# Slot tiles of a routed feed-forward layer: the up bias, the PSUM banks, the weight slots and the ring of slot rows

## Chip, core and metric

One core of a Trainium2 chip runs the program. The metric is device time of one execution in microseconds, lower is better. The engines are TensorE (PE), VectorE (DVE), ScalarE (ACT), GpSimd (POOL) and SyncE (SP); 16 DMA engines move data for all of them.

## What is computed

Four layer groups follow each other on a tensor of 8 sequences x 256 tokens x 128 features: state-space, linear, windowed, delta-rule and causal attention layers, and feed-forward layers between them. The change bears on one of these, the feed-forward layer of the first group, which the program runs twice for each half of the batch. Its shapes in the reference are

```python
B, S, H, F, E, K = (2, 256, 128, 512, 8, 2)

def _ffn(x, wi, bi, wo, bo):
    return jax.nn.selu(x @ wi + bi) @ wo + bo
```

A gate of that form (gate_wi, gate_wo) is evaluated for every token; its output picks the token's top 2 choices, and a choice below 8 names one of 8 experts with weights exp_wi (128 x 512), exp_wo (512 x 128) and biases exp_bi (512), exp_bo (128). Each chosen expert is applied to the token, and the results come back weighted. All is fp32; small bf16 operands are used where they are exact, or as three bf16 parts of one fp32 number.

## The kernel before

Everything after the inputs is held on chip. Two streams, a and b, each work on half of the sequences; stream a has PSUM banks 0 to 3, b has 4 to 7. A layer is a function that gives one generator per engine; each generator waits (`yield pe.wait_ge(signal, n)`) and issues. The planner `Weave` joins them: each engine has one instruction queue in order, and Weave picks at every step the generator that could go on first by its own due times, which come from the costs in `Lane` (L115 to L232). So a cost in `Lane` changes nothing that is computed, but the order in which the two streams' work stands on each engine, in the whole program.

`experts` is the routed layer. One call treats 8 token tiles of 128 of its stream (two sequence pairs). In steps:

- the gate, in 8 units (`GATE`), then the routing on DVE (`route`): one-hot marks, counts by a product with ones, places, the number of the expert of each of 23 slot tiles (`rows`, and `picked`, which marks in 96 rows the expert of a tile), and for each choice its `slots` row.
- POOL scatters the token rows to DRAM by `slots`, 16 indirect DMAs a stream; SP loads them back sorted by expert: `xg`, 23 tiles of 128 rows, six transfers of 4 tiles (the last of 3), all sent before the first tile.
- 23 slot tiles (`SLOT_TILES`). For tile j: `turn(q)` transposes four tiles of rows at a time into bank 3, `keep_x` on ACT copies them to `xgT`; `up(j)` makes the 128 x 512 hidden layer in bank j % 2, as four chunks of 128 columns, each a weight product and a bias product (96 rows hold three bf16 parts of the biases, in parts of 32, and `picked` chooses the expert); `grow` on ACT takes the exp, DVE makes SELU of it in two steps (`fall`, `selu`) into `hidden`; `down(j)` is four weight products and a bias product into bank 2; `keep_y` on ACT copies it out. The order on TensorE in one stream is up(j+1), down(j).
- the weights of tile j, 512 KB, come to slot j % 3 of `ring_a` or `ring_b`. SP reads the expert's number from `rows` (`value`, a TENSOR_LOAD and register steps) and sends the load for j+3 once down(j) is done.
- y goes to DRAM in groups of four tiles, POOL gathers the rows back, 16 indirect DMAs a stream, and DVE adds them to x with the weights of the choice.

`ready` prepares the bias parts once, in `m.bias16`. In the traces L148 is the line of every product, L157 of a transpose, L166 of an ACT step, L179, L182, L185 and L188 of DVE's, L216 and L221 of POOL's scatter and gather, L231 of SP's transfers.

## Time and profile before

| | us |
|---|---|
| median of 3 runs | 2962.91 (2961.7 to 2963.11) |
| the profiled execution | 2957.25 |
| its span, first to last instruction | 2955.9 |
| busy in it: PE | 2287.9 (77%) |
| DVE | 1866.6 (63%) |
| ACT | 1356.9 (46%) |
| POOL | 695.9 (24%) |

The busy times are averages over some fifteen layers with different limits. The routed layer's slot tiles run in two stretches of the span, near 384 to 560 us and 668 to 850 us. In the page's slices of 74 us these are the ones where the DMA engines are busy after the start. A busy TensorE counts as busy while its pipeline drains, so neighbouring rows overlap, and the time that one product holds the engine is the distance between two starts.

### The profile page before, as it was taken

Reading aid. Unit: us, or ns where it says so; the run is one execution under the profiler, and the core shown is the slowest. Engines: PE = TensorE matmul, PEld = TensorE weight load, DVE = VectorE, ACT = ScalarE, POOL = GpSimd, SP = SyncE. Lnnn points to the kernel's source line nnn. Section 1 sums busy time; section 2 is a strip of 40 time slices with the busy share of each in tenths; the row PEclk is TensorE's granted clock in tenths of the full one; section 3 lists DMA queues with packets and bytes.
Section 4 is the critical chain, followed back from the end, with each engine's and each line's share of the span. In section 5 each row is a group of like instructions: output and inputs, shape, how many; then the busy total and the mean of one; then the engine's idle time right before and its main releaser. Section 6 shows DMA issues by size and latency. Waiting matters only on the chain. (4 is left out here: it accounts for less than half of the span.)

```text
span 2955.9 us, 40949 instructions
## 1 busy us (share of the span) xinstructions
PE 2287.9 (77%) x15598; PEld 1476.6 (50%) x15598; DVE 1866.6 (63%) x3594; ACT 1356.9 (46%) x2546; POOL 695.9 (24%) x610
## 2 busy tenths in 40 slices
PE   4777839574948887885888689766778989779889
PEld 1222439454934544453586368445455554555554
DVE  6989824493438978879898899753562242652331
ACT  4545304231427877873652464344334333435342
POOL 2727340404042212216591066000010100100000
PEclk9989969786969998996897699778789999899899
DMA  4000047304832111110000000202000000000000
GB/s 175 0 0 1 1 134 234 99 1 152 241 93 87 43 33 40 40 33 5 0 1 1 0 1 1 70 1 68 13 1 1 1 2 1 8 1 1 1 1 7
DMA packets 70708, 117.80 MB, mean 40 GB/s; under 512 B 9616, under 2 KB 46224, under 8 KB 70160
## 3 DMA queue, kind: packets, MB, share of 16 engines
q1 hardware_dynamic: 64112, 104.69, 12.0%
q0 software_dynamic: 4096, 8.40, 0.9%
q8 instruction: 123, 2.02, 0.3%
q10 hardware_dynamic: 2304, 2.10, 0.3%
q14 instruction: 73, 0.60, 0.1%
HBM read 84.61 MB, written 16.78 MB: 34 GB/s over the span
## 5 line engine op out<-in xcount | busy, mean ns | idle before, releaser
L185 DVE SCALAR_TENSOR_TENSOR conv<-conv_in,held_l1a,conv 128x512 f32<-128x512 f32 x288 | 244.2, 871 | 29.4 <-ACT conv L166 26.4
L179 POOL TENSOR_TENSOR long<-long,product 128x512 f32<-128x512 f32 x136 | 214.1, 1593 | 198.9 <-ACT product L166 190.4
L209 POOL MEMSET wide_q<- 128x1536 f32 x8 | 11.0, 1379 | 887.1 <-DVE stream_b L182 837.3
L179 POOL TENSOR_TENSOR part<-state,c_rows 128x512 f32<-128x512 f32 x128 | 161.1, 1285 | 72.1 <-issue 53.0
L179 POOL TENSOR_TENSOR qk<-conv,held_const 128x512 f32<-128x512 f32 x64 | 92.3, 1443 | 349.4 <-DVE conv L185 349.4
L182 DVE TENSOR_SCALAR grown<-grown 128x512 f32<-128x512 f32 x92 | 39.6, 430 | 210.6 <-ACT grown L166 163.7
L148 PE MATMUL ps<-part,held_const 128*128 128x512 f32 x256 | 147.1, 659 | 13.3 <-POOL part L179 8.4
L191 DVE TENSOR_TENSOR_SCAN state<-decay,ps 128x512 f32<-128x512 f32 x128 | 146.9, 1193 | 0.0
L188 DVE TENSOR_REDUCE wide_q<-ps 128x4 f32<-128x512 f32 (+1 forms) x128 | 113.5, 950 | 49.8 <-PE ps L148 49.8
L166 ACT ACTIVATE probs<-ps 128x768 f32<-128x768 f32 x128 | 96.5, 808 | 88.2 <-PE ps L148 88.0
L148 PE MATMUL ps<-yn,nT 128*128 128x192 f32 (+2 forms) x640 | 115.6, 313 | 20.3 <-DVE yn L179 17.6
L166 ACT ACTIVATE grown<-ps,held_route 128x512 f32<-128x512 f32 x92 | 63.3, 688 | 135.1 <-PE ps L148 94.6
L179 DVE TENSOR_TENSOR x<-x,ps 128x512 f32<-128x512 f32 x44 | 30.1, 685 | 132.7 <-PE ps L148 128.3
L194 DVE COPY outT<-ps 128x256 f32<-128x256 f32 x64 | 27.0, 422 | 135.1 <-PE ps L148 134.7
L148 PE MATMUL ps<-a,held_l3f 128*128 128x512 f32 x256 | 111.7, 593 | 0.5 <-DVE a L185 0.4
L148 PE MATMUL ps<-b,held_l3f 128*128 128x512 f32 x256 | 111.3, 592 | 0.0
L148 PEld LDWEIGHTS ps<-yn,nT 128*128 128x128 f32 x640 | 95.9, 198 | 27.4 <-issue 17.9
L166 ACT ACTIVATE product<-v_in,held_l1b 128x512 f32<-128x512 f32 x136 | 92.2, 714 | 8.0 <-POOL long L179 6.1
L166 ACT ACTIVATE probs<-ps,k_inv 128x192 f32<-128x192 f32 (+1 forms) x256 | 81.2, 397 | 30.5 <-PE ps L148 28.3
L148 PE MATMUL ps<-bc,pick 96*128 96x512 bf16 x128 | 50.8, 403 | 52.2 <-DVE state L191 45.5
L157 PE MATMUL ps<-held_const,stream_a 128*128 128x128 f32 x108 | 29.3, 400 | 77.7 <-DVE stream_a L182 77.6
L166 ACT ACTIVATE c_rows<-ps 128x512 f32<-128x512 f32 x64 | 38.2, 597 | 109.7 <-PE ps L148 103.7
(503 smaller groups left out, 6135.2 us busy)
## 6 DMA issues: line engine op xcount, KB each, us to landing
ring_a<-in_experts SPq DMA_DIRECT2D x46, 512.0 KB
ring_b<-in_experts SPq DMA_DIRECT2D x46, 512.0 KB
turned<-conv SPq DMA_DIRECT2D x256, 64.0 KB
ring<-lags SPq DMA_DIRECT2D x64, 128.0 KB
held_l3f<-in_l3f SPq DMA_DIRECT2D x1, 2824.0 KB
xg<-rows_x_a SPq DMA_DIRECT2D x10, 256.0 KB
xg<-rows_x_b SPq DMA_DIRECT2D x10, 256.0 KB, 5.2
rows_y_a<-y SPq DMA_DIRECT2D x10, 256.0 KB, 5.4
```

Of the source, the lines that this page charges most:

```text
L148: ins = self.real.matmul(out, lhsT, rhs, **kw)
L157: return self.array(self.real.transpose(out, a, ident), 0.109)
L166: return self.sent(self.real.activation(out, a, func, **kw), 0.13 + columns(out) / 1150, 0.14)
L179: return self.vector(self.real.tensor_tensor(out, a, b, op), columns(out), out, a, b)
L182: return self.vector(self.real.tensor_scalar(out, a, p, q, *ops), columns(out) // 2 + 40, out, a)
L185: return self.vector(self.real.scalar_tensor_tensor(out, a, p, b, first, second), columns(out) + 60, out, a, b)
L188: return self.sent(self.real.tensor_reduce(out, a, axis, op, **kw), 0.065 + columns(a) / 960, 0.13)
L191: return self.sent(self.real.tensor_tensor_scan(out, a, b, first, one, two), 0.04 + columns(out) / 480, 0.13)
L194: return self.vector(self.real.tensor_copy(out, a), columns(out), out, a)
L209: return self.vector(self.real.memset(out, value), columns(out) // 2, out)
```

## The change

For the slot tiles of `experts`:

- The up bias is one product per tile. `lifted`, made once per call on DVE (96 x 23 x 128, bf16), is the bias table times `picked`; the table now lies with its four chunks in four rows of an expert's part (8 experts x 4 chunks = 32 rows). The product has `lifted` of tile j as its stationary operand and `chunk16`, which marks a row's chunk, spread to 512 columns, as the moving one.
- `up` and `turn` take three banks in turn, in the order in which they are used; down has bank 3. up(j+2) stands ahead of down(j), no longer up(j+1).
- `W_RING` is 4.
- `xg` is a ring of three groups of four tiles: three loads are sent ahead, the others each when the turn of the group three before it is done.
- Four costs in `Lane` are raised: scatter, gather, value, dma_start.
- `ready` splits the two bias tables apart; a group `biases` holds them and lies in the ring's memory, `route` is smaller; `m.ones` is 128 wide and takes the place of `every_row`.

```diff
     def scatter(self, table, at, a):
-        self.engine.free += 1.0
+        self.engine.free += 1.27
...
     def gather(self, out, table, at):
-        self.engine.free += 1.0
+        self.engine.free += 1.27
...
     def value(self, a, top):
-        self.engine.free += 0.3
+        self.engine.free += 0.7
         return self.real.value_load(a, min_val=0, max_val=top)
 
     def dma_start(self, out, a):
-        self.engine.free += 0.1
+        self.engine.free += 0.35
...
-W_RING = 3
+W_RING = 4
+X_RING = 3
 CHUNK = 4
-X_GROUP = [0, 0, 1, 1, 1, 1]
+STARTS = range(CHUNK, SLOT_TILES, CHUNK)
...
-               picked=([P, SLOT_TILES], BF16), slot=[P, CHOICES], miss=[P, CHOICES], slots=([P, CHOICES], U32))
+               picked=([P, SLOT_TILES], BF16), lifted=([P, SLOT_TILES, P], BF16), slot=[P, CHOICES], miss=[P, CHOICES], slots=([P, CHOICES], U32))
...
-    xg = first.place([P, SLOT_TILES, P], name="xg")
+    xg = first.place([P, X_RING * CHUNK, P], name="xg")
...
+    uses = [("turn", 0), ("up", 0), ("up", 1)]
+    for j in range(SLOT_TILES):
+        uses += [("up", j + 2)] * (j + 2 < SLOT_TILES) + [("turn", (j + 3) // CHUNK)] * (j + 3 in STARTS)
+    bank_turn, bank_up = ({k: at % 3 for at, (what, k) in enumerate(uses) if what == name} for name in ("turn", "up"))
+    freed = {use: (s.kept_x, k + 1) if what == "turn" else (s.hidden, GATE + k + 1)
+             for use, (what, k) in zip(uses[3:], uses)}
+    down_out = st.ps(3)[:, 0:P]
+    up_bank = lambda u: u % 2 if u < GATE else bank_up[u - GATE]
...
-        pe.matmul(totals, w.every_row, marks, start=True, stop=True).then_inc(s.counted)
+        pe.matmul(totals, m.ones[:, :], marks, start=True, stop=True).then_inc(s.counted)
...
         def turn(q):
             at, n = SLICES[q]
-            yield pe.wait_ge(R.x_loaded[X_GROUP[q]], 16 * X_GROUP.count(X_GROUP[q]) * (done + 1))
-            if q:
-                yield pe.wait_ge(s.kept_x, q)
+            yield pe.wait_ge(R.x_loaded[q % X_RING], 16 * (x_before[q % X_RING] + q // X_RING + 1))
+            if q == 0:
+                yield pe.wait_ge(s.slots, 1)
             else:
-                yield pe.wait_ge(s.logits, len(every))
+                yield pe.wait_ge(*freed["turn", q])
             for i in range(n):
-                mm = pe.transpose(st.tiles(3)[:, i, :], xg[:, at + i, :], m.ident)
+                mm = pe.transpose(st.tiles(bank_turn[q])[:, i, :], xg[:, q % X_RING * CHUNK + i, :], m.ident)
             mm.then_inc(s.turn)
 
         def up(j):
             W = R.ring[:, j % W_RING, :]
+            out = st.ps(bank_up[j])
             yield pe.wait_ge(s.kept_x, j // CHUNK + 1)
             yield pe.wait_ge(R.w_loaded[j % W_RING], w_at(j))
-            if j >= 2:
-                yield pe.wait_ge(s.hidden, GATE + j - 1)
-            elif j == 0:
-                yield pe.wait_ge(s.slots, 1)
-                yield pe.wait_ge(s.picked, 1)
+            if j == 0:
+                yield pe.wait_ge(s.logits, len(every))
+                yield pe.wait_ge(s.picked, 2)
+            elif j >= 2:
+                yield pe.wait_ge(*freed["up", j])
             for c in range(FC):
-                out = tile(st.ps(j % 2), c)
-                pe.matmul(out, tile(W, c), tile(b.xgT[:, j // CHUNK % 2, :], j % CHUNK), start=True, stop=False)
-                mm = pe.matmul(out, tile(m.bias16[0:SPLIT, :], c), pick(j), start=False, stop=True)
-            mm.then_inc(s.up)
+                pe.matmul(tile(out, c), tile(W, c), tile(b.xgT[:, j // CHUNK % 2, :], j % CHUNK), start=(c == 0),
+                          stop=False, skip_group_check=True)
+            pe.matmul(out.rearrange("p (c n) -> p c n", c=FC), b.lifted[0:SPLIT, j, :],
+                      m.chunk16[0:SPLIT, :].unsqueeze(2).to_broadcast([SPLIT, FC, P]), start=False, stop=True,
+                      skip_group_check=True).then_inc(s.up)
 
         def down(j):
             W = R.ring[:, j % W_RING, :]
             hidden = b.hidden[:, j % FC, :]
-            yield pe.wait_ge(s.hidden, GATE + j + 1)
             if j:
                 yield pe.wait_ge(s.y_kept, j)
             for c in range(FC):
-                pe.matmul(st.ps(2)[:, 0:P], tile(hidden, c), tile(W, FC + c), start=(c == 0), stop=False)
-            pe.matmul(st.ps(2)[:, 0:P], pick(j), tile(m.bias16[0:SPLIT, :], FC), start=False, stop=True
-                      ).then_inc(s.y_made)
+                pe.matmul(down_out, tile(hidden, c), tile(W, FC + c), start=(c == 0), stop=False)
+            pe.matmul(down_out, pick(j), m.bias_down[0:SPLIT, :], start=False, stop=True).then_inc(s.y_made)
 
         yield from turn(0)
         yield from up(0)
+        yield from up(1)
         for j in range(SLOT_TILES):
-            if j % CHUNK == 1 and j // CHUNK + 1 < len(SLICES):
-                yield from turn(j // CHUNK + 1)
-            if j + 1 < SLOT_TILES:
-                yield from up(j + 1)
+            if j + 2 < SLOT_TILES:
+                yield from up(j + 2)
+            yield pe.wait_ge(s.hidden, GATE + j + 1)
+            if j + 3 in STARTS:
+                yield from turn((j + 3) // CHUNK)
             yield from down(j)
...
         for u in range(GATE):
             yield from grow(u, m.bias_grown[:, u % FC:u % FC + 1])
         yield from keep_x(0)
         yield from grow(GATE, w.ln_alpha)
+        yield from grow(GATE + 1, w.ln_alpha)
         for j in range(SLOT_TILES):
-            if j % CHUNK == 1 and j // CHUNK + 1 < len(SLICES):
-                yield from keep_x(j // CHUNK + 1)
-            if j + 1 < SLOT_TILES:
-                yield from grow(GATE + j + 1, w.ln_alpha)
+            if j + 2 < SLOT_TILES and j + 2 not in STARTS:
+                yield from grow(GATE + j + 2, w.ln_alpha)
+            if j + 3 in STARTS:
+                yield from keep_x((j + 3) // CHUNK)
+            if j + 2 in STARTS:
+                yield from grow(GATE + j + 2, w.ln_alpha)
             yield from keep_y(j)
...
             ve.tensor_scalar(b.picked[0:SPLIT, :], b.expert[0:SPLIT, :], float(E - 1), w.own_expert[0:SPLIT, :],
                              ALU.min, ALU.is_equal).then_inc(s.picked)
+            yield ve.wait_ge(s.picked, 1)
+            ve.tensor_tensor(b.lifted[0:SPLIT, :, :], m.bias_up[0:SPLIT, :].unsqueeze(1).to_broadcast([SPLIT, SLOT_TILES, P]),
+                             b.picked[0:SPLIT, :].unsqueeze(2).to_broadcast([SPLIT, SLOT_TILES, P]), ALU.mult
+                             ).then_inc(s.picked)
             yield ve.wait_ge(*own)
             slot = step(ve.tensor_reduce(b.slot[:, :], b.running[:, :, :].rearrange("p e c -> p c e"), X, ALU.add))
...
-        yield sp.wait_ge(m.bias_ready, 6)
+        yield sp.wait_ge(m.bias_ready, 12)
         yield sp.wait_ge(s.rows, 1)
         for j in range(W_RING):
             load(j)
         yield sp.wait_ge(R.scattered, 16 * CHOICES * (done + 1))
-        for q, (at, n) in enumerate(SLICES):
-            sp.dma_start(xg[:, at:at + n, :], R.x[at * P:(at + n) * P, :].rearrange("(t p) d -> p t d", p=P)
-                         ).then_inc(R.x_loaded[X_GROUP[q]], 16)
+        def load_x(q):
+            at, n = SLICES[q]
+            to = q % X_RING * CHUNK
+            sp.dma_start(xg[:, to:to + n, :], R.x[at * P:(at + n) * P, :].rearrange("(t p) d -> p t d", p=P)
+                         ).then_inc(R.x_loaded[q % X_RING], 16)
+
+        for q in range(X_RING):
+            load_x(q)
         for j in range(SLOT_TILES):
             if j + W_RING < SLOT_TILES:
                 yield sp.wait_ge(s.y_made, j + 1)
                 load(j + W_RING)
             q = j // CHUNK
             at, n = SLICES[q]
+            if j == at and q + X_RING < len(SLICES):
+                yield sp.wait_ge(s.turn, q + 1)
+                load_x(q + X_RING)
...
-        whole = w.expert_bias[0:SPLIT, :]
         step = Steps(m.bias_ready)
-        yield step(ve.tensor_scalar(whole[:, FC * P:], whole[:, FC * P:], 1.0 / SELU_SCALE, None, ALU.mult))
-        yield step(ve.tensor_copy(m.bias16[0:SPLIT, :], whole))
-        yield step(ve.tensor_tensor(m.bias_rest[0:SPLIT, :], whole, m.bias16[0:SPLIT, :], ALU.subtract))
-        yield step(ve.tensor_copy(m.bias_mid[0:SPLIT, :], m.bias_rest[0:SPLIT, :]))
-        yield step(ve.tensor_copy(m.bias16[32:64, :], m.bias_mid[32:64, :]))
-        yield step(ve.tensor_tensor(m.bias16[64:96, :], m.bias_rest[64:96, :], m.bias_mid[64:96, :], ALU.subtract))
+        yield step(ve.tensor_scalar(w.expert_bo[0:SPLIT, :], w.expert_bo[0:SPLIT, :], 1.0 / SELU_SCALE, None, ALU.mult))
+        for whole, out in ((w.expert_bi, m.bias_up), (w.expert_bo, m.bias_down)):
+            yield step(ve.tensor_copy(out[0:SPLIT, :], whole[0:SPLIT, :]))
+            yield step(ve.tensor_tensor(m.bias_rest[0:SPLIT, :], whole[0:SPLIT, :], out[0:SPLIT, :], ALU.subtract))
+            yield step(ve.tensor_copy(m.bias_mid[0:SPLIT, :], m.bias_rest[0:SPLIT, :]))
+            yield step(ve.tensor_copy(out[32:64, :], m.bias_mid[32:64, :]))
+            yield step(ve.tensor_tensor(out[64:96, :], m.bias_rest[64:96, :], m.bias_mid[64:96, :], ALU.subtract))
+        yield step(ve.tensor_copy(m.chunk16[0:SPLIT, :], w.own_chunk[0:SPLIT, :]))
...
```

Left out: the same renaming at the places that use the banks (`grow`, `keep_x`, `keep_y`, `selu`), the memory layout and the host's tables.

What stands on TensorE in the middle of the slot tiles, where both streams run. Before, the end of an up of a, the down of a, the start of an up of b (xgT is the transposed x, ring the weights, picked with bias the bias product, hidden the SELU's output; an up has four such pairs):

```order
L148 MATMUL ps<-xgT_153,ring_a_58 128x128
L148 MATMUL ps<-picked_169,bias_9_57 128x128
L148 MATMUL ps<-ring_a_58,hidden_152 128x128 x4
L148 MATMUL ps<-bias_9_57,picked_169 128x128
L148 MATMUL ps<-xgT_470,ring_b_59 128x128
L148 MATMUL ps<-picked_486,bias_9_57 128x128
```

And now, a whole up and down of a, and of b:

```order
L148 MATMUL ps<-xgT_156,ring_a_60 128x128 x4
L148 MATMUL ps<-chunk_59,lifted_173 128x512
L148 MATMUL ps<-ring_a_60,hidden_155 128x128 x4
L148 MATMUL ps<-down_58,picked_172 128x128
L148 MATMUL ps<-xgT_475,ring_b_61 128x128 x4
L148 MATMUL ps<-chunk_59,lifted_492 128x512
L148 MATMUL ps<-ring_b_61,hidden_474 128x128 x4
L148 MATMUL ps<-down_58,picked_491 128x128
```

An up is now four products in a row and one of 512 columns; the two streams still take turns, and the up that stands ahead of a down is that of two tiles later.

On DVE, at the end of stream a's routing in the first of the two layers, before (rows is what SP reads, picked marks the experts, slot and slots lead to the scatter):

```order
L182 TENSOR_SCALAR rows_168<-expert_167 1x23
L179 TENSOR_TENSOR running_161<-running_161,onehot_160 128x128
L182 TENSOR_SCALAR picked_169<-expert_167,held_route_56 96x23
L179 TENSOR_TENSOR used_479<-running_478,held_route_56 128x64
L188 TENSOR_REDUCE slot_170<-running_161 128x16
L179 TENSOR_TENSOR weight_159<-top_154,both_156 128x16
```

And now:

```order
L182 TENSOR_SCALAR rows_171<-expert_170 1x23
L179 TENSOR_TENSOR running_164<-running_164,onehot_163 128x128
L182 TENSOR_SCALAR picked_172<-expert_170,held_route_56 96x23
L179 TENSOR_TENSOR used_484<-running_483,held_route_56 128x64
L179 TENSOR_TENSOR lifted_173<-up_57,picked_172 96x2944
L188 TENSOR_REDUCE slot_174<-running_164 128x16
```

The multiply of 2944 columns a row stands between picked and slot.

On SP, behind the first weights of both streams, in the first of the two layers, before (xg is the load of slot rows, four tiles each; rows_168 is a's table of experts):

```order
L226 TENSOR_LOAD rows_485
L226 ISA x2
L231 ISA
L231 DMA ring_b_59<-in_experts 128x1024
L231 DMA xg_175<-rows_x_a 128x4x128 x5
L231 DMA xg_175<-rows_x_a 128x3x128
L226 TENSOR_LOAD rows_168
L226 ISA x2
```

And now, where one more load of each stream stands ahead:

```order
L226 TENSOR_LOAD rows_490
L226 ISA x2
L231 ISA
L231 DMA ring_b_61<-in_experts 128x1024
L231 DMA xg_179<-rows_x_a 128x4x128 x3
L226 TENSOR_LOAD rows_171
L226 ISA x2
L231 ISA
```

a's first x loads now stand behind eight weight loads, not six, and are three, not six; the fourth follows the first weight load of the loop.

## Rows read from the trace of the kernel before

**Rows 1.** The page's first line: the span, and the instructions of all engines.

```profile
span 2955.9 us, 40949 instructions
```

**Rows 2.** Busy us by stretch: PE, PEld, DVE, ACT, POOL; PEclk, DMA share, GB/s.

```profile
411.00:441.00 30.00, 18.74 (x98) 16.96 (x99) 4.47 (x8) 4.97 (x10) 10.56 (x11) 0.64 0.46 132
441.00:530.00 89.00, 88.97 (x802) 86.42 (x800) 41.39 (x74) 40.51 (x83) 0.00 (x0) 1.00 0.79 234
```

**Rows 3.** Timeline of TensorE, one tile: start, length, engine, line, operation, out<-in, count, [idle<-releaser].

```profile
462.80 0.44 PE L148 MATMUL ps<-xgT,ring_a 128*128 128x128 f32 x2
463.08 0.22 PE L148 MATMUL ps<-picked,bias 96*128 96x128 bf16 x1
463.14 0.44 PE L148 MATMUL ps<-xgT,ring_a 128*128 128x128 f32 x2
...
464.14 1.11 PE L148 MATMUL ps<-ring_a,hidden 128*128 128x128 f32 x8
465.08 0.22 PE L148 MATMUL ps<-bias,picked 96*128 96x128 bf16 x1
```

**Rows 4.** Timeline of TensorE, products of 512 columns in bf16, first layer.

```profile
44.97 0.60 PE L148 MATMUL ps<-bc,pick 96*128 96x512 bf16 x2
...
98.98 0.38 PE L148 MATMUL ps<-bc,pick 96*128 96x512 bf16 x1
99.25 1.12 PE L148 MATMUL ps<-part,held_const 128*128 128x512 f32 x2
```

**Rows 5.** Timeline of SP's DMA issues, both stages.

```profile
429.86 3.45 SPq L231 DMA_DIRECT2D ring_a<-in_experts  x2
...
454.21 0.34 SPq L231 DMA_DIRECT2D ring_b<-in_experts  x1
...
682.78 10.60 SPq L231 DMA_DIRECT2D ring_b<-in_experts  x3
694.07 7.71 SPq L231 DMA_DIRECT2D xg<-rows_x_a  x6
```

**Rows 6.** Timeline of TensorE, places where a load or a turn is late.

```profile
433.61 0.80 PE L148 MATMUL ps<-xgT,ring_a 128*128 128x128 f32 x2 [1.41 <-DMA ring_a<-in_experts]
...
440.23 0.61 PE L157 MATMUL ps<-held_const,xg 128*128 128x128 f32 x4
...
453.13 0.22 PE L148 MATMUL ps<-bias,picked 96*128 96x128 bf16 x1
...
460.41 0.30 PEld L148 LDWEIGHTS ps<-xgT,ring_b 128*128 128x128 f32 x2 [0.26 <-DMA ring_b<-in_experts]
```

**Rows 7.** Timeline of DVE, routing of stream a, and one product of 512 elements.

```profile
381.12 0.34 DVE L179 TENSOR_TENSOR of_tile<-held_route,ends 128x184 f32<-128x184 f32 x1
...
383.62 0.16 DVE L179 TENSOR_TENSOR slots<-slot,miss 128x16 uint32<-128x16 f32 x1
...
575.94 0.70 DVE L179 TENSOR_TENSOR q<-q,peak 128x512 f32<-128x512 f32 x1
```

**Rows 8.** Timeline of POOL: a's first scatter, b's last, a's first gather.

```profile
384.07 1.44 POOL L216 DMA_INDIRECT rows_x_a<-stream_a,slots  x1 [56.21 <-DVE slots L179]
...
423.76 0.96 POOL L216 DMA_INDIRECT rows_x_b<-tok,slots  x1 [0.30 <-issue]
...
537.33 0.98 POOL L221 DMA_INDIRECT back<-rows_y_a,slots  x1 [112.61 <-DMA rows_y_a<-y]
```

**Rows 9.** Timeline of ACT, first and last steps of the first stage.

```profile
422.66 0.69 ACT L166 ACTIVATE grown<-ps,held_route 128x512 f32<-128x512 f32 x1 [11.11 <-remote]
...
554.51 0.28 ACT L166 ACTIVATE y<-ps 128x128 f32<-128x128 f32 x1 [6.42 <-remote]
560.25 0.28 ACT L166 ACTIVATE y<-ps 128x128 f32<-128x128 f32 x1 [5.46 <-remote]
```

**Rows 10.** Busy time by stretch, windowed attention, columns as in rows 2.

```profile
900.00:1100.00 200.00, 168.99 (x1140) 100.37 (x1140) 176.88 (x260) 162.94 (x378) 41.65 (x29) 0.98 0.16 39
1140.00:1340.00 200.00, 166.44 (x1085) 96.72 (x1083) 160.93 (x246) 157.87 (x361) 40.13 (x29) 0.96 0.15 38
```

39 lines of the change are left out of this document (23 added, 16 removed).

## Prediction

> **What bounds the kernel now.** I read the page first, for the span, then the busy time by stretch, then the timeline of single engines in the two places where the changed function runs. The profiled execution took 2957.25 us around a span of 2955.9 [rows 1]; the median of the runs shown is 2962.91, 5.66 more. I make the sum as a change of time and put it on the median.
>
> The slot tiles run twice, about 384 to 560 us and 668 to 850. The first is read here; the second has the same order. It has three parts. From 411 to 441 stream a runs alone, TensorE busy 18.74 of 30 us, its clock 0.64 of full, thus mostly at its lower level. From 441 to 530 both streams run, TensorE is busy 88.97 of 89 us at full clock, and the DMA engines 0.79 [rows 2]. From about 532 b runs out alone. So in the middle part TensorE's own work is the bound, and at both ends something else is: the POOL queue's scatters and gathers, the landing of weights and the way of a semaphore from one engine to the next.
>
> **The up bias product.** In the middle part one tile reads so [rows 3]: from the first up product at 462.80 to the down bias at 465.08 and 0.06 on to the next, 2.34 us. An up chunk is 0.34 (462.80 to 463.14): 0.28 for the weight product and 0.06 until the bias has made way. Counted by passes it is 12 in the up part, 1.34 us, so 0.111 each, and 9 in the down part (464.14 to 465.14), 1.00, again 0.111. The change leaves 8 passes, 0.89 us, and adds one product of 512 columns, bf16, 96 rows. The trace has that shape in the first layer: two in a row last 0.60 together where one lasts 0.38, so the second started 0.22 after the first, and one that is followed by another kind holds TensorE from 98.98 to 99.25, 0.27 [rows 4]. Up becomes 1.11 to 1.16, for 1.34: a gain of 0.18 to 0.23 a tile, and I take 0.20. How many tiles: a tile is 2.34, and a turn of four passes before every fourth tile is 4 x 0.111 = 0.45, 0.11 for each tile, so 2.45 (the turn's own row, at 440.23, has 0.61 with its drain [rows 6]); 89 / 2.45 is 36 tiles a stage, 72 in the two. 72 x 0.20 = 14.4 us, with ends 13.0 and 16.6.
>
> On this one product the Trainium skill speaks, TensorE: Matmul & The Clock Gate, section Back-to-back issue gap: it gives about 131 ns for a 512-column product in a sustained stream of weight load and product. By that figure the sum would have 0.09 more a tile, some 6 us, as an estimate from that page; the rows of this case, 0.22 and 0.27, do not agree, and I go by them.
>
> **Does the weight ring still hold?** Four slots for three sounds like one more tile of time. It is not: up now runs two tiles ahead of down, not one. Before, the load for tile j+3 is sent when down(j) has ended and is needed at up(j+3); in between stand, in TensorE's order, three tiles of the two streams (b's, a's, b's), about 3 x 2.34 + a turn = 7.0 to 7.4 us. After, the load for j+4 is sent at down(j) and needed at up(j+4), and again three tiles stand between, 3 x 2.14 = 6.4 and a turn. What it has to cover: the load goes out 1.0 us after the down bias (row at 453.13, issue at 454.21), and the longest stretch from issue to use in the middle part is 6.2, where TensorE waited 0.26 for it (460.41); the shortest, with few other transfers, is 3.75 (429.86 to 433.61, also waited for) [rows 5, 6]. 1.0 + 3.75 = 4.8 is safe in 6.4, 1.0 + 6.2 = 7.2 is not. Slack falls by 0.6 a load. The x loads add to it: before all six groups are sent before a stream's first tile, now three are, and three in the loop, on the same SP queue and DMA engines. Those are 1.5 MB for two streams on 24 MB of weights, so 6% more, at 0.79 busy. I take 3 us of waits over both stages for it; ends 0 and 14.4 (all of the gain, if loads and not TensorE set the pace).
>
> **The multiply.** New on DVE is lifted, 96 x 2944, bf16, a product of two operands that are both read with repeats. It stands in DVE's order between picked and the reduce that makes slot, thus ahead of slots, for which POOL waits with its first scatter (slots 383.62, scatter 384.07) [rows 7, 8]. POOL then works through 32 scatters, a's and b's, until 424.7 [rows 8], and the x loads, the first turn and so all of the stage stand behind them. Nothing covers it: at that time TensorE and ACT have nothing to do. Its time: of_tile has 184 elements and lasts 0.34, a 512-element product 0.70 [rows 7]; that is 1.10 ns an element, so 0.34 + 2760 x 0.0011 = 3.4 us. The rows at hand are of f32; a bf16 one at twice the speed would be 1.8. I take 3.2 for each of the two a's, 6.4 in all, ends 3.6 and 7. b's own lies behind a's scatters and costs nothing.
> The skill, VectorE: DVE Perf Modes, section What auto-detection actually checks, gives two results a cycle only where every operand is 16-bit with a step of 1; a repeated operand is not. By it the full 3.2 stands, by the opposite the sum would be 3 us better. No row here shows a large bf16 product, so this case does not decide it yet.
>
> **The start of the stage.** Stream a alone: its fourth tile waited 1.41 for its load [rows 6], since the load left only with down(0); with four slots it is there. The turn of b's first slice at 440.23 [rows 6] stands behind a's fifth up and third down; now it stands behind a sixth up and a fourth down. Followed through with the shift of 3.2, b's first turn comes about 4.2 later but with one more tile of a (2.3) done: a loss of 1.9, thus a gain of 1.3 against the 3.2. Twice: 2.6. Against it: in the second stage SP needed 10.60 us for b's three ring loads, 3.5 each (in the first, two of a's loads with the wait between took 3.45), and a's x loads, sent behind them at 694.07, took 7.71 for six [rows 5]. A fourth load there is up to 5 us more ahead of a's x loads. On the other hand ACT got a's first up only at 422.66, after 11.11 us of waiting marked remote [rows 9], so the start holds a delay that may swallow a part of a later x load. Ends for the two starts: gain 6, loss 5.
>
> **The end of the stage.** b alone is slow through the same remote waits: its last y copies came at 554.51 and 560.25, after 6.42 and 5.46 us [rows 9], while POOL gathered a's rows from 537.33 on [rows 8]. Three banks and the deeper look-ahead leave three downs instead of two behind the last up, and each down waits for the y copy before it, since the down product has one bank. I take zero, ends -3 and +3 a stage.
>
> **Edits at nothing.** The two bias splits at the start are DVE work of 96 x 128 instead of 96 x 640, while the kernel waits for its first loads; the load of the new group is smaller than what the route group loses. The count over all rows takes m.ones in place of every_row, the same product. The exp, the two DVE steps and the copies of a tile are the same instructions on the other bank.
>
> **Sum.** -14.4 + 3.0 + 6.4 - 2.6 + 0 = -7.6 us: 2962.9 - 7.6 = 2955.3, I say 2955.
>
> **Rivals.**
> *The rest of the program is put in another order.* The four raised costs of the planner (SP's dma_start and value, POOL's scatter and gather) move its due times, and with them how the two streams are interleaved in the 450 us of windowed attention and after, where nothing else is changed. The price can be read: DVE worked 176.88 of 200 us from 900 to 1100 and 160.93 of 200 from 1140 to 1340 [rows 10], the same layer with the streams interleaved in two ways. If the first half ran as the second does, it would take 176.88 / 0.805 = 220, 20 us more: 2975. If the second ran as the first, 182, 18 less: 2937. In the new order stream b's second pass ends ahead of a's, of which the last 17 of 72 tap products follow with no tap of b between; that can fill the gap behind this layer or leave DVE one stream short. Slower, and by a mechanism of its own: it decides once DVE's share in that layer falls below 0.86. I give slower 0.16, faster 0.16.
> *The loads become the bound.* If a load needs over 5.4 us from issue to landing at the new pace, each one is waited for, and the middle part stays at 2.34. Then the 11.4 that the loop was to bring are gone: 2967. For: 6.2 is there already. Against: most loads in the middle part are not waited for, and 0.79 of DMA time is used. 0.14.
> *All of it comes through.* 16.6 from the products, no waits, a multiply at the faster rate, a good start: -16.6 + 3.6 - 6 = -19: 2944. 0.14.
> *The forecast,* 2949 to 2962: 0.40.
>
> **How the numbers follow.** About 0.2% is what a measurement of this kernel can tell, 5.9 us: faster is below 2957.0, slower above 2968.8. Faster: 0.16 + 0.14 + 0.6 of the forecast's 0.40 = 0.54. Slower: 0.16, and 0.3 of the load rival, 0.20. Within: 0.26. The range for 8 in 10 runs from the faster order case to just under the slower one: 2936 to 2973.
>
> **What would show it.** The time from an up's first product to the next one's in the middle part: 2.34 should be 2.11 to 2.16. Waits of TensorE for ring_a or ring_b in that part: under 2 us a stage by the forecast, over 5 by the load rival. lifted at 3.0 to 3.4 us ahead of slots, and a's first scatter that much later. The time of b's last y copy less that of a's of_tile: 179.1 before (381.12 to 560.25 [rows 7, 9]), near 175.3 by the sum. DVE's share in windowed attention, against 0.88 and 0.80. I am wrong if the stages gain what I say and the total differs by over 8 us, which is then the order of the rest, or if the middle part is as long as before.

## The result, and the profile after

The changed kernel took 2982.07 us, median of 5 runs (2976.53 to 2985.93), the kernel before 2962.91 in the same comparison (2960.71 to 2964.69). The ratio is 1.0064, interval 1.0049 to 1.0079: 19 us slower, where 7.6 faster was forecast, and 9 above the end of the range.

The first line of the page of after, and busy time by stretch (columns as in rows 2), the same stretches as [rows 2, 10]:

```profile
span 2980.7 us, 40388 instructions
...
411.00:441.00 30.00, 18.85 (x94) 17.15 (x95) 5.60 (x10) 5.57 (x11) 12.54 (x14) 0.63 0.41 122
441.00:530.00 89.00, 85.94 (x728) 82.49 (x727) 43.50 (x78) 42.08 (x88) 2.27 (x3) 1.00 0.80 249
900.00:1100.00 200.00, 164.24 (x1098) 95.88 (x1097) 168.49 (x256) 159.26 (x368) 42.34 (x28) 0.99 0.15 38
1140.00:1340.00 200.00, 167.30 (x1067) 100.18 (x1066) 155.72 (x247) 155.28 (x349) 35.53 (x25) 0.94 0.14 33
```

Of the middle part, one whole tile of TensorE, as [rows 3]:

```profile
462.80 1.11 PE L148 MATMUL ps<-xgT,ring_a 128*128 128x128 f32 x8
463.74 0.38 PE L148 MATMUL ps<-chunk,lifted 96*128 96x512 bf16 x1
463.96 1.05 PE L148 MATMUL ps<-ring_a,hidden 128*128 128x128 f32 x8
464.85 0.22 PE L148 MATMUL ps<-down,picked 96*128 96x128 bf16 x1
464.91 1.11 PE L148 MATMUL ps<-xgT,ring_b 128*128 128x128 f32 x8
```

A tile now takes 2.11 us (462.80 to 464.91) for 2.34, and so do most: the median distance from one down bias product to the next is 2.12 for 2.34, in both stages. That is the gain that was forecast for it. Where did it go, and 19 us more? The two traces were laid beside each other at steps that both have (spans 2955.9 and 2980.7):

| | before | after | change |
|---|---|---|---|
| start to a's first of_tile | 381.1 | 378.0 | -3.1 |
| first stage, to b's last y copy | 179.1 | 174.5 | -4.6 |
| to a's of_tile of the second stage | 104.2 | 103.2 | -1.0 |
| second stage, to b's last y copy | 183.4 | 176.8 | -6.6 |
| to the first windowed step | 7.3 | 3.5 | -3.8 |
| windowed layer | 478.2 | 501.2 | +23.0 |
| on to the last product with l1b (delta rule) | 620.0 | 624.4 | +4.4 |
| the rest | 1002.5 | 1019.1 | +16.6 |

Up to 836 us the changed kernel is 19.1 ahead; behind it, where no line of the layers differs, it loses 43.9. The last three lines as stretches, after first, before second (the same columns):

```profile
836.06:1337.22 501.16, 392.64 (x2436) 228.15 (x2436) 390.49 (x611) 369.42 (x827) 111.70 (x80) 0.92 0.17 46
1337.22:1961.60 624.38, 486.86 (x2756) 357.20 (x2755) 535.72 (x844) 289.20 (x479) 269.09 (x212) 0.80 0.03 9
1961.60:2980.70 1019.10, 843.96 (x7286) 522.58 (x7285) 391.78 (x962) 394.19 (x654) 39.42 (x48) 0.92 0.03 8
```

```profile
855.21:1333.36 478.15, 382.93 (x2388) 219.37 (x2389) 380.37 (x572) 360.48 (x812) 105.35 (x78) 0.92 0.18 47
1333.36:1953.40 620.04, 475.14 (x2804) 346.36 (x2803) 545.36 (x883) 288.29 (x488) 273.28 (x212) 0.82 0.03 10
1953.40:2955.90 1002.50, 832.83 (x7286) 515.59 (x7285) 392.12 (x962) 394.73 (x655) 39.45 (x48) 0.93 0.03 8
```

DVE worked 390.5 of 501.2 in the windowed layer, before 380.4 of 478.2: share 0.78 and 0.80. Nearly all of the 10 us more of work is 39 steps of the delta-rule layer that now stand ahead of its start (x611 for x572, and x844 for x883 behind it); the rest of the 23 is idle time, 110.7 for 97.8. What DVE waits for changed as well. The wait that grew most is that of a tap product (one step of the layer's convolution) for the first tap, which ACT makes; total, times and longest, before and after:

```profile
DVE conv L185 <- ACT conv L166: 26.4, 16, 4.4
...
DVE conv L185 <- ACT conv L166: 47.4, 22, 6.2
```

The order of the windowed layer's 288 tap products on DVE tells more. a, b are the streams' first passes, A, B their second; each letter is one product, first before, then after:

```
aaaaaaaaabbbababaabaaabababbbbaababababababaabbbbbababababaaaaabbbbbbababaabaaaaabbbbbbababaabaaaaabbbbbbababaabaaaaabbbbbbababaabaaaaabbbbbbbbb
AAABABABABBABAABBBAAAABABABBABABABBBAAAABABABBABABABBBAAAABABABBABABABBBAAAABABABBABABABBBAAAABABABBABABABBBAAAABABABBABABABBBAAAABABABBABABABBB

aaaaaaaaabbbaabaababaaababbaaaaababbbabababbbaaaaababbabababbbbaaaaababbabababbbbaaaaaabababbabbbbbaaaaaabababbabbbbbaaaaaabababbabbbbbbbbbbbbbb
AAAAAAAAABBBABABBAABABBAAABBABBBBBBBAAAAAABBBBABBABABBBABBABABABABABABAABBBBBBBABBAAAABABBBABBABABBABBABABBABABABAABBBBBBBABBAAAAAAAAAAAAAAAAA
```

Before, the second pass repeats one pattern of 18. After, b is through early and a's last 17 stand alone. In that stretch, on DVE and, in the last row, ACT of after:

```profile
1300.82 0.42 DVE L179 TENSOR_TENSOR oT<-ps,inverse 128x256 f32<-128x256 f32 x1
1304.94 0.69 DVE L179 TENSOR_TENSOR x<-x,ps 128x512 f32<-128x512 f32 x1 [3.71 <-PE ps L157]
1305.66 0.87 DVE L203 BATCH_NORM_STATS2 stats<-x 128x6 f32<-128x128 f32 x4
1306.45 0.73 DVE L185 SCALAR_TENSOR_TENSOR conv<-conv_in,held_l1a,conv 128x512 f32<-128x512 f32 x1
...
1305.31 0.81 ACT L166 ACTIVATE conv<-conv_in,held_l1a 128x512 f32<-128x512 f32 x1
```

Between two of a's steps (1300.82, 1306.45) stands one of b's next layer, x, which had to wait 3.71 for TensorE. a's tap stood behind it, but its own input came from ACT only at 1306.12 (1305.31 + 0.81), so the queue held it for 0.3 at most: DVE was idle because neither of its next two steps was ready, in a place where one stream has little left to fill the other's gaps with. That this is how the whole layer gets longer is argued from such rows.

**TensorE's clock.** The three stretches also differ in the granted clock: 0.92 and 0.92 in the windowed layer, then 0.80 for 0.82 and 0.92 for 0.93. At the start of the last stretch the rows set it apart best, before first:

```profile
1953.38:2088.96 135.58, 91.54 (x1727) 70.21 (x1727) 58.40 (x151) 54.39 (x94) 0.00 (x0) 0.80 0.17 44
...
1961.58:2104.31 142.73, 98.69 (x1727) 75.41 (x1727) 57.92 (x151) 57.17 (x96) 0.00 (x0) 0.75 0.15 42
```

The same 1727 products kept TensorE busy for 7.15 us more, and the stretch is 7.15 longer. So behind the windowed layer part of the loss is not idle time but the same products at a lower clock. No run holds the clock and changes the order, so how much of the loss goes this way is read from rows and not shown by an experiment.

### The profile page after: what moved, and what is told of

Same layout as the page of the kernel before. It is cut to its first block and busy times, and to the rows that moved or that the text cites. A ratio compares the mean times of both kernels' runs of the same rounds, so it can differ in the third digit from the quotient of the medians.

```text
span 2980.7 us, 40388 instructions
## 1 busy us (share of the span) xinstructions
PE 2304.3 (77%) x15322; PEld 1491.1 (50%) x15322; DVE 1880.3 (63%) x3604; ACT 1364.0 (46%) x2550; POOL 700.3 (23%) x610
## 5 line engine op out<-in xcount | busy, mean ns | idle before, releaser
L185 DVE SCALAR_TENSOR_TENSOR conv<-conv_in,held_l1a,conv 128x512 f32<-128x512 f32 x288 | 232.5, 825 | 53.2 <-ACT conv L166 47.4
L148 PE MATMUL ps<-part,held_const 128*128 128x512 f32 x256 | 156.1, 717 | 4.7 <-POOL part L179 2.7
L148 PE MATMUL ps<-yn,nT 128*128 128x64 f32 (+2 forms) x640 | 117.6, 317 | 19.8 <-ACT nT L166 10.3
L148 PE MATMUL ps<-kT,qT 32*128 32x128 f32 (+1 forms) x1024 | 62.4, 359 | 36.0 <-DVE wide_q L188 36.0
L166 ACT ACTIVATE c_rows<-ps 128x512 f32<-128x512 f32 x64 | 38.2, 597 | 110.7 <-PE ps L148 105.2
```

What stands on the lines that cost most here:

```text
L148: ins = self.real.matmul(out, lhsT, rhs, **kw)
L166: return self.sent(self.real.activation(out, a, func, **kw), 0.13 + columns(out) / 1150, 0.14)
L185: return self.vector(self.real.scalar_tensor_tensor(out, a, p, b, first, second), columns(out) + 60, out, a, b)
```

## Experiments

The runs fell on several chips. The kernel before took 2963 and 2961 us on those of the first comparison and of runs e3 to e6, 2932 to 2934 on those of all others. Each ratio below is against before on the same chip.

### The order apart from the slot tiles

Before with the four planner costs raised; the changed kernel with them as before:

```diff
-        self.engine.free += 1.0      # scatter, gather
+        self.engine.free += 1.27
-        self.engine.free += 0.3      # value
+        self.engine.free += 0.7
-        self.engine.free += 0.1      # dma_start
+        self.engine.free += 0.35
```

> The kernel before with nothing but the four raised planner costs (scatter and gather 1.27, value 0.7, dma_start 0.35), so that only the order of the two streams' instructions changes. Theory A (the order of the rest costs the time; the slot tiles themselves gain 19 us up to the first windowed product at 836.1 against 855.2): slower than before by 20 to 50 us, near 2963 + 25 to 44 = 2988 to 3007, with windowed attention longer than its 478. Rival B (the costs hardly move the order; it is the new slot tiles' other lengths in the plan that do): within 6 us of 2963. Rival C (the changed kernel loses by the clock or by memory and not by the order): also within 6 us of 2963.

> The changed kernel with the four planner costs as before (scatter and gather 1.0, value 0.3, dma_start 0.1). Theory A (the raised costs make the bad order): the stages' gain comes through, 2963 - 19 = 2944, range 2935 to 2955. Rival B (the plan differs anyway since the slot tiles are planned differently): any order, 2950 to 2990, and then windowed attention's DVE share tells which. Rival C (no matter of order): as the changed kernel, 2982.

Measured: e1 2951.34 for 2933.29 of before, ratio 1.0064 (1.0046 to 1.0082). The costs alone, with no slot tile changed, make the kernel slower by as much as the whole change did, 18 us, which is a little under the 20 to 50 expected. e2 2921.18, 0.9961 (0.9946 to 0.9975): the slot tiles alone are 12 us faster. The two don't simply combine: 1.0064 x 0.9961 is 1.0025, and both together gave 1.0064. e1 and after have one order in the windowed layer, but not in the layers behind it (some 200 of DVE's steps stand elsewhere there), and the whole took a clock of 0.87 for 0.88; which of these makes the rest was not tried. In e2 the plan's order is that of before from the windowed layer on, but for some 45 of DVE's steps in the causal layers near the end. From the first windowed step to the end e1 took 2123.6, e2 2091.0.

Which cost is it? e3 and e4 are the two kernels unchanged; e5 raises dma_start alone on the kernel before, e6 the other three.

> The kernel before, unchanged, for a profile of it on the chip of this comparison. The chips differ: on the chip of the first two runs it took 2933.3 us. If the stage's waits marked remote are a property of the chip, the first stage's length here (first of_tile to last y copy) is not 179.1 but nearer to the 160.8 of the run with raised costs alone; if they are made by the order or the costs, it stays at 179.

> The changed kernel, unchanged, beside its variants. Theory A (slot tiles gain some 12, the new order of the rest costs some 20 to 44): ratio 1.002 to 1.009 to before, the middle part at 2.11 us a tile, and from the first windowed product to the end 20 us or more longer than in the kernel before on this chip. Rival (the loss of 19 was the first chip's): ratio under 1.000.

> The kernel before with the planner's cost of dma_start alone raised, 0.1 to 0.35. In the windowed layer 320 such issues stand on SP for lags and turned rows, so this cost moves the plan there; in order it differs from before from the first layer to the causal one. Theory A1 (this cost makes the bad order): ratio 1.004 to 1.009, 12 to 26 us slower. Rival A2 (scatter, gather and value costs make it): within 0.2% of before.

> The kernel before with scatter, gather (1.27) and value (0.7) raised and dma_start as it was. The order differs from before in the routed layers, not in the windowed one, and in some 150 DVE steps of the delta-rule layers. Theory A1: within 0.2% of before (0 to 6 us). Rival A2: 1.004 to 1.009.

| | ratio (interval) | to windowed | windowed | first windowed step to end |
|---|---|---|---|---|
| e3 before | | 859.8 | 477.5 | 2100.1 |
| e4 after | 1.0054 (1.0037 to 1.0071) | 830.2 | 500.7 | 2136.3 |
| e5 dma_start | 1.0097 (1.0072 to 1.0122) | 850.1 | 499.1 | 2136.5 |
| e6 the other three | 0.9991 (0.9975 to 1.0006) | 860.6 | 480.3 | 2096.8 |

dma_start it is: e5 has the loss of e4 from the windowed layer's start on (36.4 and 36.2) and a third of its gain ahead of it (9.7 and 29.6). Its order is not quite that of after: the windowed layer ends with 11 of a's taps alone, not 17, and 14.8 of the loss lie in the delta-rule layer, where e4 loses 3.9. The first stage took 178.3 in e3, not something near the 160.8 of e1, which by what was expected of e3 speaks for the order or the costs, and not the chip, as what makes ACT's waits marked remote. e11 below corrects that: the kernel before, unchanged, on one more chip took 159.7 and shows none, and on the chip of e3 to e6 all four show them, whatever their costs.

### What the slot tiles gain

e7 repeats e2. e8 has four bias products again, in a row, planned as one, so that nothing moves:

```diff
-            pe.matmul(out.rearrange("p (c n) -> p c n", c=FC), b.lifted[0:SPLIT, j, :],
-                      m.chunk16[0:SPLIT, :].unsqueeze(2).to_broadcast([SPLIT, FC, P]), start=False, stop=True,
-                      skip_group_check=True).then_inc(s.up)
+            for c in range(FC):
+                mm = pe.real.matmul(tile(out, c), b.lifted[0:SPLIT, j, :], m.chunk16[0:SPLIT, c:c + 1].to_broadcast([SPLIT, P]),
+                                    start=False, stop=(c == FC - 1), skip_group_check=True)
+            pe.array(mm, FC * P / 2400).then_inc(s.up)
```

> The changed kernel with the four planner costs of before, a second time, as the kernel that the next three are compared with. Expected: ratio 0.996 to before, the windowed layer's taps in 456 to 460 us, middle part 2.11 us a tile. Against it: that the 12 us of the first time were that chip's, whose waits marked remote were absent; then the ratio is 0.999 or more.

> As the run with the old costs, but the up bias is again four products of 128 columns (lifted of the tile against one marked column each), planned as one of 512, so that the order is the same. Theory (the one product gives 0.2 a tile): middle part 2.32 to 2.36 a tile, total 10 to 16 us over the run with the old costs. Rival (loads or semaphores set the pace): under 5 us over.

Measured: e7 2917.75 for 2933.99, 0.9944 (0.9922 to 0.9966); e8 2918.27, 0.9948 (0.9926 to 0.9970). The expectation of 10 to 16 us between them failed. TensorE of e8, as [rows 3]:

```profile
457.25 1.11 PE L148 MATMUL ps<-xgT,ring_a 128*128 128x128 f32 x8
458.08 0.33 PEld L824 LDWEIGHTS ps<-chunk,lifted 96*128 96x128 bf16 x4
458.19 0.39 PE L824 MATMUL ps<-chunk,lifted 96*128 96x128 bf16 x4
458.43 1.11 PE L148 MATMUL ps<-ring_a,hidden 128*128 128x128 f32 x8
459.37 0.22 PE L148 MATMUL ps<-down,picked 96*128 96x128 bf16 x1
459.43 0.77 PE L148 MATMUL ps<-xgT,ring_b 128*128 128x128 f32 x5
```

A tile is 2.18 (457.25 to 459.43), not 2.34: four bias products in a row hold the engine for 0.24, one of 512 for 0.22, and the down behind them takes 1.00 and not 0.95. What was saved is for the most part not three products of four, nor their loads, of which there are still four, but their place between the weight products: there each fp32 weight product holds the engine for 0.28 (462.80 to 463.08 [rows 3]), here for 0.235 (a quarter of 457.25 to 458.19). e8 also keeps the new roles of the two operands, which were not tried apart. 0.06 to 0.07 a tile over 72 tiles would be 4 to 5 us; the two stages together are 4.3 longer than in e7 (157.5 + 156.4 against 154.8 + 154.8), and the totals don't separate them.

e9 puts the multiply behind slots:

```diff
+            ve.tensor_tensor(b.slots[:, :], b.slot[:, :], b.miss[:, :], ALU.add).then_inc(s.slots)
             yield ve.wait_ge(s.picked, 1)
             ve.tensor_tensor(b.lifted[0:SPLIT, :, :], m.bias_up[0:SPLIT, :].unsqueeze(1).to_broadcast([SPLIT, SLOT_TILES, P]),
...
-            ve.tensor_tensor(b.slots[:, :], b.slot[:, :], b.miss[:, :], ALU.add).then_inc(s.slots)
```

> As the run with the old costs, but the multiply lifted stands behind slots on DVE, so that the scatters don't wait for it; its order in the first windowed pass is the same. Theory (the multiply stands on the path): of_tile to slots 2.5 us, not 5.6, in stream a, and 4 to 7 us less in total. Rival (the scatters of b or waits marked remote end later anyway): within 2 us of the run with the old costs.

Measured: 2948.25, 1.0042 (1.0021 to 1.0063), 30 us over e7. Its order in the delta-rule layers is another one; of the 35 lost from the windowed layer on, 24 are lost there and later, and 11.5 in the windowed layer, whose taps stand as in e7. The stages themselves took 154.4 and 153.3 (e7: 154.8, 154.8), a gain of 2 and not 6. DVE's two multiplies and POOL's scatters beside them in e9:

```profile
383.62 3.21 DVE L179 TENSOR_TENSOR lifted<-up,picked 96x2944 bf16<-96x2944 bf16 x1
...
388.92 3.21 DVE L179 TENSOR_TENSOR lifted<-up,picked 96x2944 bf16<-96x2944 bf16 x1
...
383.98 4.04 POOL L216 DMA_INDIRECT rows_x_a<-stream_a,slots  x1 [56.91 <-DVE slots L179]
388.32 0.97 POOL L216 DMA_INDIRECT rows_x_a<-stream_a,slots  x1 [0.30 <-issue]
389.59 3.38 POOL L216 DMA_INDIRECT rows_x_a<-stream_a,slots  x1 [0.30 <-issue]
```

Scatters that begin beside a multiply last 4.04 and 3.38; the one between them 0.97, and the first of before, which is longer than the others, 1.44 [rows 8]. In after the same is to be seen:

```profile
379.81 3.21 DVE L179 TENSOR_TENSOR lifted<-up,picked 96x2944 bf16<-96x2944 bf16 x1
...
383.63 0.16 DVE L179 TENSOR_TENSOR slots<-slot,miss 128x16 uint32<-128x16 f32 x1
...
385.50 3.22 DVE L179 TENSOR_TENSOR lifted<-up,picked 96x2944 bf16<-96x2944 bf16 x1
...
384.08 1.42 POOL L216 DMA_INDIRECT rows_x_a<-stream_a,slots  x1 [57.26 <-DVE slots L179]
385.80 3.76 POOL L216 DMA_INDIRECT rows_x_a<-stream_a,slots  x1 [0.31 <-issue]
...
426.53 0.96 POOL L216 DMA_INDIRECT rows_x_b<-tok,slots  x1 [0.30 <-issue]
```

The scatter that started at 385.80, 0.30 into b's multiply, took 3.76; its neighbours take 0.96. From first to last scatter it was 39.69 before (384.07 to 423.76 [rows 8]) and is 42.45. So b's multiply is not free, and moving the multiply behind slots only exchanges a later first scatter for a longer one. The Trainium skill, SBUF — State Buffer, section Who interferes with whom, has this: a VectorE instruction with two SBUF inputs contends with a GpSimd instruction that reads SBUF, and the order of issue decides which one is blocked. The trace agrees: the scatter, second to start, ended at 389.56, 0.84 behind the multiply (385.50 + 3.22 = 388.72). The same section also tells of a probe in which tensor_tensor did not stall a DMA; for this kernel's indirect ones the traces say otherwise.

e10 looks one tile ahead again, with all else as in e7:

```diff
-            if j + 2 < SLOT_TILES:
-                yield from up(j + 2)
+            if j + 3 in STARTS:
+                yield from turn((j + 3) // CHUNK)
+            if j + 1 < SLOT_TILES:
+                yield from up(j + 1)
             yield pe.wait_ge(s.hidden, GATE + j + 1)
-            if j + 3 in STARTS:
-                yield from turn((j + 3) // CHUNK)
```

> As the run with the old costs (planner costs as before), but TensorE looks one tile ahead as before: up(j+1) ahead of down(j), turn ahead of up. The plan then gives the windowed layer the irregular order with stream a's last 17 tap products alone, though no cost is raised. Theory A (the order, not the costs' numbers, costs the time): windowed taps in 474 to 480 us, and from the first windowed product to the end 25 us or more longer than in the run with the old costs. Rival (something else in the raised costs): 456 to 460. Slot tiles: the stage itself within 4 us of the run with the old costs if the look-ahead is worth little, as the prediction had it.

Measured: 2963.52, 1.0080 (1.0052 to 1.0107). The windowed part took 503.5 (e7: 472.7), the whole from there to the end 2154.4 for 2092.2, with no cost raised. And the stages took 148.7 and 148.6, some 6 less than with the look of two: here the second tile of look-ahead costs. The ten executions are not alike: six took 2962.88 to 2973.98 at a granted clock of 0.866 to 0.875, four 2944.57 to 2947.95 at 0.878 to 0.885. The trace is of the longest.

e11 and e12 are before and e2 again, for two profiles of one chip.

> The kernel before, unchanged, for a profile beside the next kernel on the same chip. The stage from a's first of_tile to b's last y copy took 179.1 and 178.3 on two chips with waits marked remote on ACT; on the chips of the last four runs these are absent and the changed slot tiles took 152.7 to 154.8. If the chip makes the difference, this is 179 where the next kernel has 168 to 172, or 160 to 164 where the next has 155.

> The changed kernel with the planner costs of before, beside a profile of the kernel before on the same chip. Expected: from first windowed product to the end within 10 us of before, and both stages together 10 to 20 us shorter; ratio 0.994 to 0.997. If the chip has the remote waits, the gain is in the stage's start and end too and not smaller.

Measured: e11 2928.47 (before 2932.09 in all its runs), e12 2921.59, 0.9961 (0.9948 to 0.9975). Stages 159.7 and 164.8 before, 153.5 and 156.4 in e12: 14.6 less. At the start of the windowed layer 5.9 are left (829.1, 823.2): from b's last y to a's next of_tile it took 110.0 in e11 and 117.5 in e12, so half of the gain is given back between the stages.

### The same slot tiles in two orders

e13 and e14 have e10's slot tiles. They differ in one number, found by trying planner costs until the plan gave before's order again from the windowed layer on (in DVE's queue but for some steps at its start, two taps among them that change places, and 5 later ones):

```diff
-        self.engine.free += 1.0      # scatter, gather (e14)
+        self.engine.free += 1.1      # e13
```

> The slot tiles that look one tile ahead (one up bias product, four slots, three banks, planner costs as before), with one cost set by hand: scatter and gather 1.1 instead of 1.0, at which the plan gives from the windowed layer on the order of the kernel before. The same slot tiles with the irregular order were 1.0080 times before. Theory A (the order of the rest is the whole loss): the slot tiles took 148.7 us a stage there, 6 less than with the look two tiles ahead, and the rest 2091 us with this order: ratio 0.991 to 0.995 to before, 35 us or more below the same tiles with the irregular order. Rival (the slot tiles that look one ahead carry the loss themselves): 1.000 or more.

> The kernel with the irregular order, unchanged, on the same chip as its twin with the regular one. Theory A: again 1.005 to 1.011 to before, with the first windowed product to the end 40 to 62 us longer than in the twin.

Measured: e13 2921.02, 0.9951 (0.9931 to 0.9972); e14 2960.79, 1.0072 (1.0042 to 1.0102). The three stretches from the first windowed step on (columns as before), e13, then e14:

```profile
815.20:1299.10 483.90, 385.07 (x2388) 221.51 (x2389) 381.15 (x572) 359.83 (x812) 100.29 (x74) 0.92 0.18 46
1299.10:1918.30 619.20, 473.08 (x2803) 345.89 (x2802) 543.13 (x883) 288.59 (x488) 271.05 (x212) 0.82 0.03 10
1918.30:2917.80 999.50, 829.24 (x7287) 513.25 (x7285) 392.36 (x962) 394.43 (x655) 39.44 (x48) 0.94 0.03 8
```

```profile
817.10:1314.70 497.60, 391.23 (x2436) 228.86 (x2436) 392.41 (x612) 366.70 (x827) 102.17 (x74) 0.92 0.17 45
1314.70:1953.50 638.80, 499.93 (x2757) 366.00 (x2756) 541.10 (x844) 294.46 (x483) 270.70 (x212) 0.78 0.03 9
1953.50:2965.60 1012.10, 841.92 (x7285) 520.10 (x7283) 392.48 (x962) 396.81 (x656) 39.47 (x48) 0.92 0.03 8
```

Both reach the windowed layer alike, 815.2 and 817.1; then e14 needs 14, 20 and 13 us more. That settles the cause: the order of the rest, with the same slot tiles and the same work, is worth 40 us between the medians.

How it costs them differs by layer. In the windowed layer, DVE's taps wait for ACT's first tap 24.8 to 29.6 us in the ten traces that have before's order there but for a few steps, and 36.5 to 53.8 in the six that have an irregular one (27.4 in e13, 36.5 in e14). Behind it, it is TensorE's time: in e14 it is busy 26.8 and 12.7 longer than in e13, DVE 2.0 less and then the same, and the clock is 0.78 for 0.82 and 0.92 for 0.94. The single executions agree. e13's ten took 2909.48 to 2927.72 at a clock of 0.880 to 0.889. Of e14's six, two took 2938.66 and 2940.78 at 0.883, and four 2957.99 to 2967.17 at 0.869 to 0.873. So every one of e14 is longer than every one of e13; at a like clock the irregular order costs some 19 us, and in most executions it comes with a lower clock and some 25 more. All nine of after and e4 lie at 0.868 to 0.874.

e13's time from the first windowed step on, 2102.6, came out 12 us above the 2091 expected, and its ratio at the upper end of what was expected (0.995). Its first windowed pass of a took 213.4, and there b's first tap stood 36.0 behind a's (819.0, 855.0), where it was 27.7 in e7 (a's pass 204.6), 27.9 in e11 (204.4), 31.9 in e3 (208.6) and 37.4 in e9 (213.5). The order begins with nine taps of a and three of b, so what a stage gains for a alone can be waited away there. DVE's longest wait for turned rows is 11.2 in e13 and e9, and 4.4 in e7. No run tried this apart.

e2, e7, e12 and e13 all beat both kernels, by 0.4 to 0.6% to before. Between them the intervals overlap.

## Why the prediction was wrong, step by step

**The step that failed** is the one that made the sum of the stage's terms the sum of the program. It stood among the rivals (the rest of the program is put in another order), with 0.16 for slower and 0.16 for faster, and a price for the windowed layer alone, 20. The mechanism is that rival's and its price for that layer was right, 23.0; but the layers behind it, where the order is new too, lost 21.0 more, and no term stood for them. In the sum itself the rest of the program was put at nothing, and it measured +43.9. DVE's share, its decision point, was 168.49 of 200 from 900 to 1100, 0.84, under the 0.86 that it named. The diff names dma_start, which stands in 320 transfers of the windowed layer for lags and turned rows: the prediction says itself how the new order ends, with 17 of the tap products in a row, so the chance of a new order was near 1, and the 0.32 could only divide between worse and better. That it would be worse could not be read from the trace. But that case's own time, 2975, lay outside the range given (2973), and with the 21.0 of the later layers it would have been 2996, past the 2982 measured. What the rival had wrong is that a lower share of DVE is the whole price: behind the windowed layer the longer time is TensorE's, at a lower clock.

**The up bias product**: right in size. 2.11 a tile for a forecast of 2.14; half clock or contention did not enter. Its reason was half right (e8): 0.16 of the 0.23 come from grouping, 0.07 from one product for four. The figure of 131 ns for a 512-column product, from the Trainium skill, TensorE: Matmul & The Clock Gate, section Back-to-back issue gap, was not reached; the step from it to the next product is 0.22 (463.74 to 463.96).

**The weight ring**: 3 us of waits were put in. TensorE's waits for the ring add up to 2.7 in the first stage and 4.9 in the second; before to 5.8 and 6.4. So the term was a gain of 4.6, with its sign wrong; loads were no bound. All but 0.5 of these waits lie at the two ends of the stages (before from 433.61 [rows 6] on, in after at 530.51 and 533.43), not where both streams run, so some of the 4.6 is also in the terms for start and end.

**The multiply**: 3.21 each, as forecast (3.2). But the claim that b's own costs nothing failed: it held a scatter for 2.8 more in the first stage and 2.1 in the second (3.08 for 0.96). The term is 11.3 and not 6.4. e9 shows no cheap way round it.

**Start and end.** Rows of after: SP's issues of b's four ring loads in the second stage and a's first x loads, TensorE's first turn of b, the last y copies of b in the first stage.

```profile
677.22 4.65 SPq L231 DMA_DIRECT2D ring_b<-in_experts  x4
687.47 1.51 SPq L231 DMA_DIRECT2D xg<-rows_x_a  x3
...
441.43 0.61 PE L157 MATMUL ps<-held_const,xg 128*128 128x128 f32 x4
...
544.93 0.28 ACT L166 ACTIVATE y<-ps 128x128 f32<-128x128 f32 x1 [7.07 <-remote]
549.92 0.28 ACT L166 ACTIVATE y<-ps 128x128 f32<-128x128 f32 x1 [4.71 <-remote]
552.53 0.28 ACT L166 ACTIVATE y<-ps 128x128 f32<-128x128 f32 x1 [2.33 <-PE ps L148]
```

b's four loads took 4.65 to issue, and not more than the 10.60 for three [rows 5], so that fear was void. b's first turn came 14.90 after the last scatter (426.53 to 441.43), before 16.47 (423.76 to 440.23): a gain of 1.6, forecast 1.3. At the end the remote waits are 7.07 and 4.71 for 6.42 and 5.46 [rows 9], zero as forecast. From of_tile to the last y it is 174.5, forecast 175.3. For the stages of these two traces, then, forecast and trace are near each other: -7.6 by the sum, -11.2 by the traces. With -16.3 for the products (72 x 0.226), -4.6, +11.3 and -3.2 the terms as measured give -12.8; that this is so near is in part luck, since the ring and the multiply were off by 7.6 and 4.9 in opposite directions. On other chips the stages gained more, 16.6 (e3, e4) and 14.6 (e11, e12).

**What was not thought of**: gains of a stage are not carried whole to the next fixed place in the order (e12: 7.5 of 14.6 lost between the stages), and the same tiles gain 6 more a stage with the shorter look-ahead (e10, e13).

## What to carry to other kernels

Where a planner sets the order from costs, a changed cost is an edit of the whole program: compare the order far from the edit, and before judging a local change, hold the rest to its old order (by the old costs, or by a cost that gives it back) and time the two apart. Read a local gain in the trace between two steps of that place, not from the total; here a total of +19 hid a gain of 10 to 16 (e2, e7, e12). Look at each execution's granted clock beside its time: one kernel's ten executions fell into two groups by it (e10), and a single trace shows only one of them. And an instruction that has an idle engine to itself may still stand in another's way, as the multiply did for the scatters.

## What the runs showed of the hardware

- A VectorE product of two operands of 2944 elements a row held GpSimd's DMA_INDIRECT: 3.76 and 3.08 (after) and 3.38 us (e9) for 0.96, 4.04 (e9) for the first one's 1.4.
- Four bf16 products of 128 columns in a row on one stationary operand hold TensorE for 0.24, one of 512 columns 0.22; each in turn with fp32 products added 0.06 and made those longer, 0.28 for 0.235 (before, e8).
- The bf16 multiply with repeated operands ran at 1.09 ns an element (3.21 / 2944), the rate of fp32. The Trainium skill, VectorE: DVE Perf Modes, section What auto-detection actually checks, gives such an instruction a faster mode only if every tensor is 16-bit with a step of 1, and a repeated operand has none; the trace agrees.
- The same products in the same number at a lower granted clock: 1727 of them kept TensorE busy for 98.7 us at 0.75 and 91.5 at 0.80, and the stretch grew by the same 7.15. One kernel's executions split by the clock: 2963 to 2974 us at 0.866 to 0.875, 2945 to 2948 at 0.878 to 0.885 (e10). What decides which of the two an execution gets stays open.
- ACT's waits marked remote go with the chip: on two of them the first stage of before, which has them there, took 179.1 and 178.3, on another, without them, 159.7. What delays them there was not tried and stays open, as does which feature of the irregular order costs most.
